# Gate rows through DRAM on ScalarE's queue, mask constants on GpSimd's, and the two groups' gate math at other steps

## The reference

```python
x = x + mlstm(layernorm(x), ctx, ctx, igate, fgate, outnorm_weight)
x = x + moe(layernorm(x), w12, w3, gate_w)

def mlstm(q, k, v, ...):                       # 8 heads of 32 features
    ig = concat(q, k, v) @ igate_kernel + igate_bias      # one number per token and head
    fg = concat(q, k, v) @ fgate_kernel + fgate_bias
    cs = cumsum(log_sigmoid(fg))
    log_D = where(tril, cs[s] - cs[t] + ig[t], -inf)
    m = max_t(log_D);  C = (q . k / sqrt(32)) * exp(log_D - m)
    h = C / (max(|sum_t C|, exp(-m)) + 1e-6) @ v
    return head_layernorm(h) * outnorm_weight

def moe(x, ...):                               # 8 experts, the best 2 per token
    p = softmax(top2(x @ gate_w.T))
    return sum_e p_e * (silu(x @ w1_e) * (x @ w2_e)) @ w3_e
```

## Time and profile before

| | |
|---|---|
| median of three runs | 682.49 us (681.91 to 683.64) |
| the profiled execution, its own time | 679.7 us |
| its span | 678.0 us |
| PE, DVE, ACT, POOL busy | 84%, 69%, 49%, 46% |
| PE's share in the slices of the first 120 us | from a third to nine tenths, changing |
| DMA | 66.87 MB, mean 99 GB/s; 245 GB/s in the first slice of 17 us |
| mean granted TensorE clock | 0.917 of full speed |

### The profile page before, as it was taken

How to read it: one execution, slowest core, us unless ns; L and a number is a source line. 1 busy time by engine, 2 the same in 40 slices (tenths; PEclk the granted TensorE clock), 3 DMA queues, 4 the chain that set the end, 5 groups by cost and what they waited for, 6 DMA issues and landing times.

```text
span 678.0 us, 14645 instructions
## 1 busy us (share of the span) xinstructions
PE 570.1 (84%) x3612; PEld 470.5 (69%) x3613; DVE 469.3 (69%) x987; ACT 335.4 (49%) x745; POOL 310.0 (46%) x316
## 2 busy tenths in 40 slices
PE   3867689989899864023999999999999999999993
PEld 1333567878778753012888888888888888888882
DVE  4572177888787887994676767677777767676763
ACT  2535255666667643201555555555555555555551
POOL 3312235556556550502355545454555555454532
PEclk9979578999999985555999999999999999999998
DMA  7763344455555433802233333333232333333332
GB/s 245 231 188 105 102 114 137 149 169 171 156 189 162 147 109 115 326 3 45 33 59 53 54 56 50 60 48 62 47 63 47 58 52 55 55 54 56 49 46 24
DMA packets 61148, 66.87 MB, mean 99 GB/s; under 512 B 12146, under 2 KB 55034, under 8 KB 61116
## 3 DMA queue, kind: packets, MB, share of 16 engines
q0 software_dynamic: 15552, 25.21, 20.4%
q1 hardware_dynamic: 36860, 32.88, 16.1%
q10 hardware_dynamic: 8704, 8.39, 3.5%
HBM read 43.24 MB, written 18.75 MB: 91 GB/s over the span
## 4 chain that ended last, share of the span: by engine, by line
issue 41%; DVE 19%; PE 13%; POOL 13%; DMA 8%; SPq 3%; ACT 2%; DVEq 0%; POOLq 0%; ACTq 0%
POOL xg L1127 8%; DMA out_rows<-ys,index 6%; PE bank L1246 5%; POOL out_rows L1136 4%; PE dots L1228 3%; DVE c L822 3%; DVE ohn L969 2%; DVE tot L863 2%; DVE ohp L968 2%; DVE st L701 2%; DVE mu L858 1%; PE dots L1179 1%; PE dots L1181 1%; DVE wden L859 1%; DVE wabs L857 1%
## 5 line engine op out<-in xcount | busy, mean ns | idle before, releaser
L1136 POOL DMA_INDIRECT out_rows<-ys,index x71 | 112.9, 1590 | 154.7 <-DVE ys L1021 143.5
L1027 DVE TENSOR_TENSOR w3l<-w,w3h 128x1024 fp32r<-128x1024 f32 x71 | 87.1, 1227 | 31.0 <-issue 30.0
L1127 POOL DMA_INDIRECT xg<-token_table,index x71 | 70.4, 992 | 51.8 <-DVE index L986 29.9
L667 ACT CAST w3h<-w 128x1024 fp32r x71 | 74.4, 1048 | 20.3 <-issue 20.3
L1246 PE MATMUL bank<-aug,c 128*128 128x99 f32 (+2 forms) x512 | 67.4, 288 | 15.7 <-DVE c L822 15.6
L1246 PEld LDWEIGHTS bank<-aug,c 128*128 128x128 f32 x512 | 63.6, 202 | 21.9 <-DVE c L822 20.1
L1368 PE MATMUL bank<-w3l,hth 128*128 128x256 f32 x284 | 76.5, 302 | 1.8 <-DVE w3l L1027 1.8
L1369 PE MATMUL bank<-w3h,hth 128*128 128x256 f32 x284 | 70.8, 282 | 0.0
L1021 DVE TENSOR_SCALAR ys<-bank,pc 128x256 f32<-128x256 f32 x71 | 34.3, 484 | 46.6 <-PE bank L1372 46.6
L1004 DVE TENSOR_TENSOR htl<-bank,hth 128x512 fp32r<-128x512 f32 x71 | 49.1, 691 | 25.1 <-ACT hth L657 25.1
L1340 PE MATMUL weighs<-w12l,xh 128*128 x144 | 62.0, 431 | 1.1 <-DVE xl L993 1.1
(11 more groups left out here) (165 smaller groups left out, 1246.9 us busy)
## 6 DMA issues: line engine op xcount, KB each, us to landing
wst<-in_w12T POOLq DMA_DIRECT2D x24, 256.0 KB, 3.6
aug<-in_ctxv SPq DMA_DIRECT2D x16, 264.0 KB, 3.7
w12h<-in_x SPq DMA_DIRECT2D x16, 256.0 KB, 2.9
w12l<-in_ctxT SPq DMA_DIRECT2D x16, 256.0 KB, 3.4
qbd<-w12h SPq DMA_DIRECT2D x64, 64.0 KB
x<-in_x SPq DMA_DIRECT2D x16, 256.0 KB, 2.8
out_rows<-x ACTq DMA_DIRECT2D x16, 256.0 KB, 2.1
token_table<-x2n ACTq DMA_DIRECT2D x16, 256.0 KB, 2.4
```

The lines of the kernel that those rows point to most:

```text
L667: nc.scalar.copy(W3H[i][:], w3[:, bass.ds(e, 1)].rearrange("p a k d -> p (a k d)")).then_inc(w3h_ready, 1)
L1027: v.tensor_tensor(W3L[i][:], w3[:, bass.ds(e, 1)].rearrange("p a k d -> p (a k d)"), W3H[i][:].bitcast(F32), ALU.subtract).then_inc(w3l_re ...
L1127: q.indirect_dma_start(out=XG[x][:], out_offset=None, in_=table, in_offset=bass.IndirectOffsetOnAxis(ap=index[:, j:j + 1], axis=0)).then_i ...
L1136: q.indirect_dma_start(out=out, out_offset=bass.IndirectOffsetOnAxis(ap=index[:, j:j + 1], axis=0), in_=YS[o][:], in_offset=None, compute_ ...
```

## The change

The gate rows no longer go from SBUF to SBUF on SP's queue. ScalarE issues one DMA for each sequence, one loop turn after it has copied the rows, and writes all 16 of them to DRAM (`gate_scratch`); `pair_gates` on SP fetches a whole group with two DMAs. The six mask DMAs of each buffer are issued by GpSimd at b = 2 and 4. SP loads queries, AUG and KN of sequences 0 and 1 inside the gating loop (b = 12 to 15) and their gate rows right behind it. Group 0's math moves from b = 8, 10, 11 to b = 9 to 14 in smaller pieces; group 1's moves from step 1 to step 0 on VectorE, and up within step 0 on ScalarE. `pair_rows(1)` moves from the end of step 3 to the end of step 2.

```diff
+    gate_dram = nc.dram_tensor("gate_scratch", (B, 2 * NH, S), F32).ap()
...
+            def pair_gates(part):
+                rows_ = (AHEAD, REST)[part]
+                lo, hi = ((0, LEAD), (LEAD, B))[part]
+                for i in range(2):
+                    sp.wait_ge(gate_out[i], 8 * hi)
+                for k, dst in enumerate((gi, gf)):
+                    sp.dma_start(dst[rows_, :], gate_dram[lo:hi, k * NH:(k + 1) * NH, :]).then_inc(pair_in, 16)
...
-            for b in range(B + 5):
-                old = b - 5
+            for b in range(B + 1):
...
-                if b in (9, 11):
-                    mask_constants((b - 9) // 2)
-                if 0 <= old:
-                    sp.wait_ge(gates_ready, old + 1)
-                    at = (old - LEAD) % B * NH
-                    for k, dst in enumerate((gi, gf)):
-                        sp.dma_start(dst[at:at + NH, :], GS1[old % 2][k * NH:(k + 1) * NH, :]
-                                     ).then_inc(gate_out[old % 2], 16)
-                if b == B:
-                    pair_rows(0)
+                if b == 10:
+                    pair_gates(0)
+                if b in (12, 13):
                     sp.wait_ge(zeroed, 1)
-                    load_queries(0, 0)
-                if b == B + 1:
-                    sp.wait_ge(parts_out, 16 * (1 + PARTS))
-                    load_gates(0, 0)
+                    load_queries(b - 12, b - 12)
+                if b in (14, 15):
+                    load_values(b - 14, b - 14)
+            pair_rows(0)
+            sp.wait_ge(parts_out, 16 * (1 + PARTS))
+            for b in range(2):
+                load_gates(b, b)
+            pair_gates(1)
...
+                if isinstance(b, int) and b == LEAD - 2:
+                    pair_rows(1)
                 if isinstance(b, int) and b == LEAD - 1:
-                    pair_rows(1)
...
                     act.wait_ge(gates_psum, a_ + 1)
-                    wait(act, gate_out[i], 16 * (a_ - i))
+                    wait(act, gate_out[i], 8 * (a_ - i))
                     nc.scalar.copy(GS1[i][:], bank[2 + i][0:2 * NH, 0:S]).then_inc(gates_ready, 1)
+                if has(b, 3):
+                    a_ = b - 3
+                    act.wait_ge(gates_ready, a_ + 1)
+                    act.dma_start(gate_dram[a_], GS1[o][:]).then_inc(gate_out[o], 16)
...
-                for i in range(2):
-                    act.wait_ge(gate_out[i], 16 * (LEAD, B)[part])
+                act.wait_ge(pair_in, 32 * (part + 1))
...
-                if b == 8:
+                if b == 9:
                     act.wait_ge(late_consts, 16 * N_LATE)
                     forget(0)
                 if b == 11:
-                    gate_parts(0, 0, 2)
+                    gate_parts(0, 0, 1)
+                if b == 12:
                     decays(0)
-                if b == 12:
+                if b == 13:
+                    gate_parts(0, 1, 2)
+                if b == 14:
                     gate_parts(0, 2, 3)
...
                 if has(b, 0):
                     weights(b, 1)
+                if isinstance(b, int) and b == 0:
+                    forget(1)
...
-                if b == 8:
+                if b == 10:
                     preactivation(0)
-                if b == 10:
+                if b == 11:
                     maxima(0)
-                if b == 11:
-                    three_parts(dve, v, negM, AHEAD, m_parts, 0)
+                if b == 12:
+                    three_parts(dve, v, negM, AHEAD, m_parts, 0, 0, 2)
+                if b == 13:
+                    three_parts(dve, v, negM, AHEAD, m_parts, 0, 2, 3)
...
-                    if c == 1 and isinstance(b, int) and b == 1:
-                        preactivation(1)
-                        maxima(1)
...
                 if has(b, 0):
                     combine(1)
+                if isinstance(b, int) and b == 0:
+                    preactivation(1)
+                    maxima(1)
...
+                if b in (2, 4):
+                    mask_constants(b // 2 - 1)
```

60 lines of the change are left out of this document (29 added, 31 removed).

## The result

The changed kernel takes 676.37 us (median of 4 runs, 675.01 to 676.94), the kernel before in the same session 682.2 (4 runs, 681.37 to 683.64). The ratio, taken over all runs and not as the quotient of the two medians, is 0.9909 with an interval of 0.9887 to 0.9932: faster by 5.8 us, 0.9%. Forecast were 13.5 us and 669.0. The range of 663.5 to 677.5 holds the time, but of the gain that was forecast only 5.8 us came.

A forecast was written before the change was run, and what follows sets the result against it. Stalls and low clock before step 4, in the first 123 us, were to shrink: gating 2.6, hand-over 2.7, step 0 5.4, steps 1 to 3 2.8, together 13.5 us off 682.5, giving 669.0 us, range 663.5 to 677.5.

The forecast's parts named there:

- Steps 1 to 3: Mixing steps 1 to 3 at 11.1, 11.9 and 10.8 us, 33.8 for 36.6 before, all at full clock: gain 2.8.
- stick out by about 0.8: Group 1's 3.6 us of preactivation and maxima mostly fit VectorE's free end of step 0, and exceed it by 0.8 us.
- hidden: In step 2, SP's moved pair_rows(1) and 5.5 us of issues behind it delay nothing; exponents due at 8 us, queries 11.9.
- Gating: Gating up to turn 15: 59.3 us for 61.92 before, a gain of 2.6 us.
- the first mask set at 0.65: Start of the gating: some 420 KB of masks at b = 2 delay x by 0 to 1.4 us, taken as 0.65.
- the landing of a store at 2.4: ScalarE's gate stores land in 2.4 us, just under a stage, so no copy waits; 3.65 us would use up the gain.
- Hand-over: From gating to mixing: first scores 0.7 us after the gating ends, where 3.4 passed before; gain 2.7 us.
- Step 0: First mixing step: 11.1 us for 16.5, with KV waiting only about 1.2 us for GpSimd's low and vw; gain 5.4.
- a low clock and new waits in the first steps: Rival: clock stays low in the new first steps or new waits stick out; 675 us, 17 in 100.
- signs of being wrong: Gate copies waiting for gate_scratch, clock near 0.5 in steps 0 to 2, GpSimd DMAs over 1 us, steady step not 10.4.
- GpSimd's DMAs held up: Rival: VectorE delays GpSimd's mask DMAs; 671.5 us, or 681 at 3.1 us for each; 5 in 100.
- the stores: Rival: ScalarE's stores pace the gating; 674 us at a 3.0 landing (4 in 100), 709 at 5.7; beyond 3.65, 4 in 100.

The follow-up runs named there:

- the run with the split: Changed kernel with four gate buffers, group 1's preactivation kept in step 0 and its maxima moved to step 1: 669.28 us.
- all with late masks: Changed kernel with four gate buffers, maxima in step 1, pair_rows(1) ending step 3, low of step 2 later, both mask sets at b = 10: 665.76 us, quickest.

## Why the prediction was wrong, step by step

**The step that failed is the term "Steps 1 to 3"**, put at 33.8 us. They took 41.8. That is 8.0 of the 8.3 us that are missing at step 4 (13.5 forecast, 5.2 measured): the term was to gain 2.8 us and lost 5.2. It has two places, step 1 with 3.9 us and step 2 with 3.5; step 3 adds 0.6, mostly by the half clock with which it begins. In both, something was taken to be hidden that was not.

*Step 1: group 1's math was to "stick out by about 0.8".* The step took 14.95 us for 11.1. Three sizes were off. The rows were taken to land 3 us and 3 us after the gating, 5.3 after the first scores; the last store took 2.85 to land and the fetch of 96 rows 4.27, one after the other, and with the issue between them they came 8.1 after. The math was taken as 3.6 us; it was 5.6 (73.89 to 79.5), since VectorE waited 1.16 for `forget` and the scan took twice its time beside GpSimd. And the free end of step 0, measured as busy time in a step that was then 16.5 us long, was no longer there in a step of 9.8: I used the old step's gap for the new step's work. Together TensorE waited 3.76. The second half of the price I had in a rival only: the wait put TensorE at the half clock. Against the run with the split the step lost 5.3 us, 2.75 by the longer wait and the rest, some 2.5, by matmuls at that clock. The runs with the math back in step 1 (3.8 us less, and 6.1 with four buffers) confirm the place.

*Step 2: `pair_rows(1)` "hidden".* It was not. SP wrote its three parts in 3.15 us from 90.19 on and issued the queries from 95.14 to 97.85, and TensorE waited 2.96 for them. The prediction had sequence 3's exponents due 8 us into the step and its queries only at 11.9, with its scores. But in the kernel the exponents of the first half wait for all of in3, and that counts the gate rows and the four queries together (LOADS3 = 3 + HG):

```python
def exponents(b, i, c):
    if c == 0:
        pe.wait_ge(in3[i], loaded(b, i, LOADS3))
...
def load_queries(b, i):
    for j in range(HG):
        ...
        sp.dma_start(QBD[i][rows_, :, j, :], kept(flat_h, b)[rows_]).then_inc(in3[i], 16)
```

So the queries were due with the exponents. By the prediction's own 1.5 us, 5.5 us of issue and 2.4 of landing that is a wait of about 1.4 us, and not hidden; measured, the exponents were due 7.3 us into the step (97.80) and started at 100.76. But this alone decided nothing, as the run without it shows. Behind it stood VectorE, whose `wabs` was held for 3.8 to 4.4 us until the end of GpSimd's row of instructions. The kernel before had this hold too, 1.95 and 1.71 us in steps 2 and 3; in its timeline I had not looked at it, and counted steps 2 and 3 near the steady one. The steady step has it as well: in ten of them `wden`, the next small instruction, takes 1.68 us, before and after the change, and it ends with `low` (127.58 and 127.53 in the kernel before). That is inside its 10.4 us. Step 2's 15.4 us are 4.65 of waits (1.07 for vw, 2.96 for the queries, 0.62 for c) and 10.8 of TensorE's work. The same work takes 8.5 in the quickest kernel, whose granted clock over this step is 1.00, so 2.3 are the half clock.

What decides between a step 2 of 12.2 (four buffers and math in step 1; all with late masks) and one of 15 to 16 is not settled. Both short ones have a `wabs` under 2 us, value products of the second half at the full clock (1.97 us), and no wait for queries; so has step 2 of the kernel before, with 12.7 us and 1.95. A `wabs` under 2 us alone is not enough: with the math back in step 1 and two buffers it is 1.73, the value products take 3.41 at the half clock, and the step 13.9. Whether the shorter hold keeps the clock up, or the clock shortens the hold by moving what stands beside it, no run tells apart.

**Gating: 1.0 us for 2.6.** Right were the stall at turn 10 and its cause (3.90 for 3.5) and the pace of the stages behind (turn 10 to 15 in 15.95 us, forecast 16.9). Wrong was the first mask set at 0.65: it cost 2.8 us at turn 4. The pace of 2.78 us for a stage was right where the masks were away: with them at b = 6 and 8, turns 2 to 9 took 19.4 us, forecast 19.5, and 23.0 in the changed kernel. I had reckoned with its bytes at the rate of a filled stretch and put the delay at turn 2; that turn was early. The x that was late was that of sequence 4, for which VectorE stood ahead of turn 3. It was issued at 13.11, 1.2 us later than before and while the last of the set was still under way (the rows issued near 8.2 took 7.0 and 7.8 us), and it took 5.99 us where it took 3.9 before. The slow stage that followed was missing from the sum too. The end of my range for it was 1.4, so this was outside. Also wrong was the landing of a store at 2.4, "just under a stage, so no wait". Its median of 2.8 was the upper of the rows, its longest 4.2, beyond the 3.65 us named as the deciding landing for all stages; it waited in five turns, for 6.0 us in all, and 1.1 reached the first scores in the pair of traces, 1.5 in the mean of all of them. The rest lay in slack. Too strong was also the reading of the kernel before: the 1.72 us for which its gate copy waited are less than a third of the 5.89 us in front of L734; the rest is what else stood ahead of `forget(0)` on ScalarE, and forget itself.

The Trainium skill (DMA: Bandwidth & Descriptors) has the fixed part of a DMA at about 2.0 us (section "Anatomy of one DMA") and says that it is smaller where DRAM is less loaded (section "Latency and other measured facts"). The trace agrees with the direction: of the sixteen stores of 16 KB, nine had a DMA share of 0.67 or more in the 3 us behind the issue and landed after 2.3 to 4.2 us, five had 0.14 to 0.49 and landed after 1.4 to 2.2; the last two, at 0.07, took 3.0 and 2.9 and don't fit. What was waited for was the spread, not the median.

**Hand-over: right.** 4.8 us from turn 15 to the first scores, forecast 4.9, before 7.6. The run with the rows from SBUF to SBUF takes 7.5 (60.66 to 68.14).

**Step 0: right in what it waits for, 1.3 us better.** 9.8 us for 11.1; KV waited 1.43 for GpSimd. The clock was full, and none of the stalls of the earlier trace rows is left.

**The rivals.** What came is the first, a low clock and new waits in the first steps, which had 675 us and 17 in 100; it named other places (KN of step 3 and the gate rows of the hand-over, neither of which was waited for). Of its signs of being wrong, gate copies that wait for `gate_scratch` came, and low clocks in steps 1 and 2; the first scores at 65.76 were outside its 63 to 65, and turn 3 had over 2 us of idleness in front beside turn 10. VectorE did wait for `forget`: 3.0 us for group 0, which its own sum had though its list of signs had not, and 1.16 for group 1. The steady step stayed at 10.4. Of the second, GpSimd's DMAs held up, nothing is seen: its twelve mask DMAs took 0.49 to 0.64 us each. The Trainium skill has 3.1 us for such an issue beside a VectorE copy (SBUF — State Buffer, section "A bandwidth-pool intuition that's wrong", and the box on "The DVE blocks DMA trap" for the condition). None of GpSimd's here took that long. Another rule of that page of the Trainium skill fits: VectorE and GpSimd share a pair of ports, which one instruction holds for its whole length, and a VectorE instruction with two inputs in SBUF competes for it with a GpSimd instruction that reads SBUF (section "Who interferes with whom"). The prediction did not use it. It shows on the shortest ones, `wabs`, `wden` and `least`, and the trace goes further than the rule: they waited not for one instruction of GpSimd's but mostly for the last of a row of them. That the shared ports are the cause is inferred from the ends that meet; the runs show only that the hold moves when GpSimd's instructions move. Third, the stores: they were waited for in five turns, and with four buffers the median is 2.4 us lower; they did not pace the whole gating.

## What to carry to other kernels

The room for work that is moved must be read in the step as it will be, not as it is: an edit that takes stalls out of a step also takes the gaps that the next edit wants to use. A transfer waited for is to be costed by its slowest landing under the load of its place, and two landings one after the other count twice. When a stall goes after an edit and the time doesn't change, look at what stands next to it before judging the edit: `pair_rows(1)` and VectorE's hold covered one another, and taking the first off alone gained nothing. And before a transfer is called hidden, the semaphore that its reader waits for must be looked up: one that counts several transfers makes the last of them due with the first use.
